# A graph network kernel whose gathers are paced by GpSimd: two halves of each round fetched row by row by SyncE and ScalarE

## The reference

```python
def _round(x, w, b, gamma, beta, src, dst, etype):
    h = jax.nn.relu(_bn(x, gamma, beta))          # N x 128
    h = jnp.einsum('nd,od->no', h, w) + b         # N x 640, one message row for each of 5 types
    msg = h.reshape(N, T, D)[src, etype]          # 200,000 rows of 128 floats
    return jax.ops.segment_sum(msg, dst, num_segments=N)
h_new = _round(features, w1, b1, g1, be1, src, dst, etype)
h_new = _round(h_new, w2, b2, g2, be2, src, dst, etype)
```

## Time and profile before

| | |
|---|---|
| median of 3 runs | 6475.83 us (6472.38 to 6478.03) |
| the profiled execution | 6482.43 us, of which its span is 6480.6 us |
| mean granted clock of TensorE | 0.727 |
| busy | POOL 71%, PE 64%, DVE 59%, ACT 25% |
| round 0: first to last gather | 164.4 to 2061.2 us |
| round 1: first to last gather | 2181.8 to 4074.4 us |
| second layer | from about 4085 us to the end |

### The profile page before, as it was taken

How to read it: one execution, slowest core, us unless ns; L and a number is a source line. 1 busy time by engine, 2 the same in 40 slices (tenths; PEclk the granted TensorE clock), 3 DMA queues, 4 the chain that set the end, 5 groups by cost and what they waited for, 6 DMA issues and landing times. The chain is left out here.

```text
span 6480.6 us, 66649 instructions
## 1 busy us (share of the span) xinstructions
PE 4158.0 (64%) x17271; PEld 2806.2 (43%) x17271; DVE 3822.2 (59%) x7438; ACT 1611.9 (25%) x3872; POOL 4619.0 (71%) x4787
## 2 busy tenths in 40 slices
PE   7445454544445645455454555778777889999898
PEld 4333343433334434334343444333323346666696
DVE  6544444443334777776676666544444457777698
ACT  4000000000001200000000000576666656666504
POOL 5777777777777677777777777577777777777604
PEclk9555555555556755655555676898898889999999
DMA  9211121212223521221222333333333356777696
GB/s 342 53 52 52 52 53 52 52 52 55 65 65 117 188 52 52 53 52 52 52 52 53 86 90 92 99 117 110 110 110 110 110 174 217 220 219 216 208 315 211
DMA packets 432604, 726.45 MB, mean 112 GB/s; under 512 B 104654, under 2 KB 206576, under 8 KB 431506
## 3 DMA queue, kind: packets, MB, share of 16 engines
q1 hardware_dynamic: 281652, 400.74, 19.7%
q0 software_dynamic: 150592, 321.58, 17.0%
HBM read 509.16 MB, written 212.75 MB: 111 GB/s over the span
## 5 line engine op out<-in xcount | busy, mean ns | idle before, releaser
L573 POOL DMA_INDIRECT edge_rows<-messages,idx_stage x1504 | 1446.1, 961 | 487.1 <-issue 457.9
L1658 PE MATMUL banks<-onehot,edge_rows 128*128 128x128 f32 x3008 | 715.9, 413 | 995.7 <-DMA edge_rows<-messages,idx_stage 960.8
L1658 PEld LDWEIGHTS banks<-onehot,edge_rows 128*128 128x128 f32 x3008 | 613.8, 303 | 1117.2 <-DMA edge_rows<-messages,idx_stage 1082.0
L630 POOL DMA_INDIRECT sorted_rows<-edge_rows,idx_stage x784 | 760.3, 970 | 276.3 <-issue 238.2
L630 POOL DMA_INDIRECT sorted_rows<-buf_a,idx_stage x784 | 760.5, 970 | 260.5 <-issue 241.4
L573 POOL DMA_INDIRECT buf_x<-messages,idx_stage x747 | 717.4, 960 | 227.7 <-issue 227.7
L573 POOL DMA_INDIRECT buf_a<-messages,idx_stage x747 | 714.5, 957 | 227.7 <-issue 227.7
L1040 DVE TENSOR_TENSOR buf_a<-buf_a,banks 128x128 f32 x375 | 108.1, 288 | 1044.3 <-PE banks L1658 1005.4
L689 ACT ACTIVATE h_stage<-banks,bn_shift,bn_scale 128x128 f32<-128x128 f32 x128 | 58.6, 458 | 2521.1 <-PE banks L1599 2521.1
L1658 PE MATMUL banks<-x_onehot,buf_x 128*128 128x128 f32 x1494 | 355.9, 413 | 490.6 <-DMA buf_x<-messages,idx_stage 490.5
L1658 PE MATMUL banks<-x_onehot,buf_a 128*128 128x128 f32 x1494 | 344.8, 403 | 459.9 <-DMA buf_a<-messages,idx_stage 459.5
(11 more groups left out here) (201 smaller groups left out, 7088.3 us busy)
## 6 DMA issues: line engine op xcount, KB each, us to landing
buf_a<-sorted_rows SPq DMA_DIRECT2D x593, 288.0 KB, 4.0
messages<-work SPq DMA_DIRECT2D x196, 320.0 KB
buf_a<-dst_rows SPq DMA_DIRECT2D x198, 256.0 KB
buf_a<-in_attr SPq DMA_DIRECT2D x198, 128.0 KB, 2.5
buf_a<-h_in SPq DMA_DIRECT2D x396, 64.0 KB
edge_rows<-messages,idx_stage POOLq DMA_INDIRECT x1504, 2.5
sorted_rows<-edge_rows,idx_stage POOLq DMA_INDIRECT x784
sorted_rows<-buf_a,idx_stage POOLq DMA_INDIRECT x784
```

What stands on the lines that cost most here:

```text
L573: nc.gpsimd.indirect_dma_start(gathered[p][h][:, t, :], None, source, bass.IndirectOffsetOnAxis(ap=idx_stage[:, h, t:t + 1], axis=0),).the ...
L630: nc.gpsimd.indirect_dma_start(sorted_rows, bass.IndirectOffsetOnAxis(ap=idx_stage[:, 2 * u + h, t:t + 1], axis=0), msg_halves[2 * u + h][ ...
L1658: last = nc.tensor.matmul(ps_sums[p][slot][j], rows_in_slot[:, j * GROUP_TILES + t, :], hot[:, j * GROUP_TILES + t, :], start=(t == 0), st ...
```

## The change

In each round, halves 140 and 141 (`FETCHED`) are not gathered by POOL. SP fetches half 140 and ACT half 141, each with one DMA for each of its 1,024 rows of 512 bytes, into two buffers of their own. Both load the row numbers from `msg_idx` four at a time. SP does its half in one go behind the stores of the messages; ACT does two partitions' rows (16 DMAs) after each of its 64 raw tiles. PE waits for the fetched half's own semaphore where it comes to it. Since the new buffers of round 1 take the place of `f_sb`, the memset of its last row and the loads of the attributes move to iteration 74 of round 1. A few semaphores are merged, with their counts carried on.

```diff
+FETCHED = (2 * 70, 2 * 71)
...
+        def fetch_tile(engine, kind, p, i, e, t):
+            rows = table[p].rearrange("n (t d) -> (n t) d", t=T)
+            at = nc.values_load_multi_w_load_instructions(
+                msg_idx[e:e + 1, FETCHED[i] * HALF_TILES + t:FETCHED[i] * HALF_TILES + t + 4], engines=[kind], min_val=0,
+                max_val=N * T - 1, skip_runtime_bounds_check_because="a source times the types plus a type")[1]
+            for j in range(4):
+                engine.dma_start(fetched[p][i][e:e + 1, t + j, :], rows[ds(at[j], 1), :]).then_inc(s_fetched[p][i], 16)
...
+            def fetch_half(p):
+                sp.wait_ge(s_setup, RANGE_LINKS + 2)
+                for q in range(SLOTS):
+                    sp.wait_ge(s_row_out[q], rows_out(p, q))
+                for e in range(P):
+                    for t in range(0, HALF_TILES, 4):
+                        fetch_tile(nc.sync, mybir.EngineType.SP, p, 0, e, t)
...
                 for n in range(TRANS_ITERS * SLOTS, BLOCKS):
                     store_messages(n, n % SLOTS)
 
+                fetch_half(rnd)
                 if rnd == 0:
 
                     sp.wait_ge(s_bias_split, 5)
...
             load_x(0)
+            sp.wait_ge(s_y, 1)
+            load_x(1)
             for h in range(2):
                 load_attributes(h, h)
-            sp.wait_ge(s_y, 1)
-            load_x(1)
...
                         pool.wait_ge(s_idx[p], r * GATHER_SLOTS + (h + 1))
+                        if r * GATHER_SLOTS + h + 2 * RAW_ITERS[p] in FETCHED:
+                            continue
...
+                act.wait_ge(s_setup, RANGE_LINKS + 2)
+                for q in range(SLOTS):
+                    act.wait_ge(s_row_out[q], rows_out(rnd, q))
                 for t in range(RAW_ITERS[rnd] * ITER_TILES):
...
                     nc.scalar.activation(h_stage[:, t % 2, :], ps_raw_turned, ACT.Relu,
                                          bias=bn_shift[:, 0:1], scale=bn_scale[:, 0:1]).then_inc(s_raw_h, 1)
+                    for e in range(2 * t, 2 * t + 2):
+                        for first in range(0, HALF_TILES, 4):
+                            fetch_tile(nc.scalar, mybir.EngineType.Activation, rnd, 1, e, first)
...
-                    pe.wait_ge(s_gather[2 * u + h][j], gathers(p, 2 * u + h, j, turn + 1))
+                    if source is None:
+                        pe.wait_ge(s_gather[slot][j], gathers(p, slot, j, turn + 1, after or isinstance(r2, int) and r2 > FETCH_TURN))
+                    else:
+                        pe.wait_ge(s_fetched[p][source], FETCH_ROWS)
```

More of the change, by code:

```diff
@@ L95 @@
 assert all(n % 2 == 0 and (2 * HALF_TILES // 2 + 1) * n + HALF_TILES + 2 <= CHUNK_ITERS + RAW_TILES for n in RAW_ITERS)
+assert RAW_TILES == P // 2
+assert all(2 * max(RAW_ITERS) <= k < 2 * CHUNK_ITERS for k in FETCHED)
 assert X_COLS * X_PARTS == N and X_COLS % BN_CHUNK == 0 and GROUPS % 4 == 0
@@ L194, in gnn_program @@
         raw_rows = [c[:, 0:RAW_TILES * P].rearrange("p (t n) -> p t n", n=P) for c in (buf_x, buf_a)]
+        fetched = [[c.rearrange("p (t n) -> p t n", t=HALF_TILES) for c in (
+            spare[:, at + half_cols * (2 + i):at + half_cols * (3 + i)] for i in range(len(FETCHED)))]
+            for spare, at in ((buf_x, RAW_ITERS[0] * ITER_TILES * P), (buf_a, RAW_ITERS[1] * ITER_TILES * P))]
         row_stages = [buf_a[:, i * WIDE:(i + 1) * WIDE] for i in range(6, CHUNKS)] + [
@@ L282, in gnn_program @@
         s_parts_in, s_bias_split = sem("bias_rows_in"), sem("bias_split")
-        s_bn, s_bn_sd = [sem(f"bn_step_{i}") for i in range(2)], [sem(f"bn_sd_{i}") for i in range(2)]
+        s_bn, s_bn_sd = [sem(f"bn_step_{i}") for i in range(2)], sem("bn_sd")
         s_h_ready = [sem(f"h_ready_{i}") for i in range(2)]
@@ L287, in gnn_program @@
         s_row_out = [sem(f"rows_out_{q}") for q in range(SLOTS)]
-        s_clear = [sem(f"acc_cleared_{i}") for i in range(2)]
+        s_clear = sem("acc_cleared")
         s_idx = [sem(f"idx_ready_{i}") for i in range(3)]
         s_gather = [[sem(f"gathered_{h}_{j}") for j in range(2)] for h in range(GATHER_SLOTS)]
+        s_fetched = [[sem(f"fetched_{p}_{i}") for i in range(len(FETCHED))] for p in range(2)]
         s_onehot = [sem(f"onehot_ready_{i}") for i in range(2)]
@@ L306, in gnn_program @@
         s_ps_iota, s_first = sem("iota_in_psum"), sem("first_places_step")
-        s_hot = [sem(f"high_onehot_{i}") for i in range(2)]
+        s_hot = sem("high_onehot")
         s_count, s_paired, s_picked, s_passed, s_placed, s_placed_out = (sem(n) for n in (
@@ L321, in gnn_program @@
         s_prod, s_turned = sem("products_ready"), sem("products_turned")
-        s_tagged, s_part = sem("rows_tagged"), sem("partitions_in_psum")
+        s_tagged = sem("rows_tagged")
         s_scat = [sem(f"scattered_{i}") for i in range(MSG_SLOTS)]
@@ L347, in rows_out, with gathers @@
             return ((each if stores is None else stores) + (1 + rnd * each)) * 16
-        def gathers(p, h, j, n):
+        def gathers(p, h, j, n, after=False):
             missing = 0 if h < GATHER_SLOTS - 1 else GROUP_TILES - LAST_TILES if j == 0 else GROUP_TILES
@@ L352, in gathers @@
             done = n * GROUP_TILES - (missing if isinstance(n, int) and n == turns_of[p] else 0)
-            return (done + p * (turns_of[0] * GROUP_TILES - missing)) * 16
+            skipped = GROUP_TILES * len([k for k in FETCHED if k % GATHER_SLOTS == h])
+            return (done + p * (turns_of[0] * GROUP_TILES - missing - skipped) - (skipped if after else 0)) * 16
+        FETCH_ROWS = COLS_HALF * 16
+        FETCH_TURN = FETCHED[0] // GATHER_SLOTS
+        assert all(k // GATHER_SLOTS == FETCH_TURN for k in FETCHED)
+        def fetch_tile(engine, kind, p, i, e, t):
[5 more added lines that the diff above has]
+                engine.dma_start(fetched[p][i][e:e + 1, t + j, :], rows[ds(at[j], 1), :]).then_inc(s_fetched[p][i], 16)
         def turns(engine, first, end, rolled=False):
@@ L418, in _ @@
             sp.wait_ge(s_short_out, 32)
-            for q in range(SLOTS):
-                sp.wait_ge(s_row_out[q], rows_out(1, q))
             def load_x(m):
@@ L610, in _ @@
             gather_raw(0)
-            nc.gpsimd.memset(buf_a[:, :], 0.0).then_inc(s_clear[0], 1)
+            nc.gpsimd.memset(buf_a[:, :], 0.0).then_inc(s_clear, 1)
             for rnd in range(2):
@@ L617, in _ @@
                     pool.wait_ge(s_closed, 2)
-                    nc.gpsimd.memset(buf_x[:, :], 0.0).then_inc(s_clear[1], 1)
+                    nc.gpsimd.memset(buf_x[:, :], 0.0).then_inc(s_clear, 1)
                 gather_pass(rnd, table[rnd].rearrange("n (t d) -> (n t) d", t=T),
@@ L668, in _ @@
                 act.wait_ge(s_bn[rnd], N // BN_CHUNK + 1)
-                nc.scalar.activation(bn_tmp[:, 0:1], bn_mv[:, 1:2], ACT.Sqrt, bias=eps_col[:, 0:1]).then_inc(s_bn_sd[rnd], 1)
+                nc.scalar.activation(bn_tmp[:, 0:1], bn_mv[:, 1:2], ACT.Sqrt, bias=eps_col[:, 0:1]).then_inc(s_bn_sd, 1)
                 act.wait_ge(s_bn[rnd], N // BN_CHUNK + 5)
@@ L888, in batch_norm @@
                 link(nc.vector.bn_aggr(bn_mv[:, :], bn_cols[rnd]))
-                dve.wait_ge(s_bn_sd[rnd], 1)
+                dve.wait_ge(s_bn_sd, rnd + 1)
                 dve.wait_ge(s_const_in, CONSTANTS * 16)
@@ L932, in build_high @@
                     src_high[:, ds(it * ITER_TILES + h * HALF_TILES, HALF_TILES)].unsqueeze(2).broadcast_to(shape),
-                    ALU.is_equal).then_inc(s_hot[p], 1)
+                    ALU.is_equal).then_inc(s_hot, 1)
             def count_lanes(k, h, j, i):
-                dve.wait_ge(s_hot[0], k + 1)
+                dve.wait_ge(s_hot, k + 1)
                 dve.wait_ge(s_count, k * 2 + (j + 1))
@@ L946, in pair_lanes @@
             def pair_lanes(k, h, i):
-                dve.wait_ge(s_hot[1], k + 1)
+                dve.wait_ge(s_hot, k + (2 * ITERS + 2))
                 dve.wait_ge(s_passed, k + (i + 1))
@@ L1259, in count_round, with filter_ones @@
                             round_half(0, buf_a, r, u, h, None, bases, False)
+            def filter_ones():
+                nc.vector.memset(f_sb[RBF:RBF + 1, :, :, :], 1.0).then_inc(s_cut, 1)
             def rank_beyond():
@@ L1266, in rank_beyond @@
                 dve.wait_ge(s_acc[1], GROUPS - 1 - 4 * RAW_ITERS[1] + SUMS)
+                filter_ones()
                 y_chunk(0)
@@ L1294, in round_pass @@
             def round_pass(p):
-                dve.wait_ge(s_clear[p], 1)
-                if p == 1:
-                    nc.vector.memset(f_sb[RBF:RBF + 1, :, :, :], 1.0).then_inc(s_cut, 1)
+                dve.wait_ge(s_clear, p + 1)
                 dve.wait_ge(s_row_ready[p], BLOCKS + SLOT3)
@@ L1437, in _ @@
             y_chunk(CHUNKS_IN)
-            nc.vector.tensor_copy(ps_part, part_f[:, :]).then_inc(s_part, 1)
+            nc.vector.tensor_copy(ps_part, part_f[:, :]).then_inc(s_ps_iota, 1)
             stage_cutoff(0, 0)
```

(18 more changed lines are left out.)

## The result

The changed kernel takes 6992.3 us (median of 6 runs, 6988.01 to 6996.79) against 6475.2 us before (median of 6, 6472.38 to 6478.03): ratio 1.0799, 95% interval 1.0789 to 1.081. It is 517 us slower; 7000 was forecast, 6955 to 7290 as the range. The profiled execution took 6996.8 us, 6995.0 of it span.

A forecast was written before the change was run, and what follows sets the result against it. POOL's gathers, 1.26 us apart, were taken to bound the kernel. A stall of + 564.5 us less 40.3 for saved gathers made + 524.2: 7000 us against the median, range 6955 to 7290.

The forecast's parts named there:

- The place of the loss: Round 0: PE waits for bias rows behind SP's fetch, POOL stops after 32 staged gathers; net + 524.2 us.
- Its size: Round 0: POOL's 33rd gather starts at 770.9 and not at 206.4, 564.5 us late.
- The term of SP's length: SP's round 0 fetch: 256 groups take 594 us, from 164.4 to 758.4.
- the chain of 12.5 us: Round 0: from SP's bias-row issue through PE's first sum to the copy staging half 12, 12.5 us.
- The price of a group: SP's fetch: one register load and four one-row DMAs with their register instructions take 2.32 us.
- the signs that the prediction named: Among them, on SP: register loads of 0.3 us, DMAs of 0.28 to 0.35 us, bias rows near 758.
- The gain: POOL, both rounds: 32 gathers fewer at 1.26 us, 40.3 us saved, 20.2 in each round.
- The argument for it: Round 0: half 142's row numbers are staged 6 us before POOL starts half 140, so the whole 40.3 us counts.
- The rivals: Faster or a tie, 0.02 and 0.01; dearer ACT fetches, 8580 us, 0.05; fetches waiting to land, about 11,800, 0.05.
- Fetches that follow one another only when landed: Rival on SP and ACT: each row takes 2.5 us, total about 11,800 us; chance 0.05.
- Faster: Rival: SP's 256 groups take under 70 us together, down to 6436 us; chance 0.02.
- Round 1: SP's fetch hidden, done near 2776 before half 140 is due at 3515; gathers' stretch 20 us shorter, no idle.

The follow-up runs named there:

- the version without a stall: SP's three bias-row loads put ahead of its round 0 fetch, all else as in the changed kernel: 6434.2 us, ratio 0.9938.
- the first two experiments: Against the changed kernel: bias-row loads ahead of SP's round 0 fetch, 6434.2 us; PE's wait for them moved to the last layer's output, 6432.8 us.

## Why the prediction was right

**The place of the loss.** As forecast: PE waits for `bias_rows` behind 1,024 fetches, POOL runs out of staged halves after 32 gathers. Shown by two runs that move one end of this wait each and lose the stall whole, and by one that halves it.

**Its size.** 564.5 us were forecast, 557.0 measured. The term of SP's length, 594 us, was 586.6 (register load at 163.84 us to the end of the last fetch at 750.4); the start and the chain of 12.5 us were right to 0.6 us.

**The price of a group was right by luck.** It was put together from a register load of 0.302 us and a DMA of 0.31. The lines of the changed kernel:

```profile
L369 SPq TENSOR_LOAD <-msg_idx x256: 457/561/731, 163.8 to 747.9; - x128
...
L373 SPq DMA_DIRECT2D buf_x<-messages x1024: 224/225/336, 164.5 to 750.2; - x171
```

The load is 0.26 us longer than its row of before, + 66 us over 256 groups. The DMA is 0.085 us shorter than the value taken, and shorter than each of the rows it was taken from the earlier trace rows, - 87 us. Slower first DMAs of a group (0.26), a few long loads and slightly longer gaps bring back some 13. So of the signs that the prediction named, neither the loads of 0.3 us nor the DMAs of 0.28 to 0.35 us came. Both prices came from the nearest rows, and each was wrong by more than a quarter. A better row for the load stood beside the one taken: the 0.531 us of DVE, which the prediction priced at 59 us more. The Trainium skill ("DMA: Bandwidth & Descriptors", section "Latency and other measured facts") names some 600 ns as the least for a register load; the prediction set this against the 302 ns on SP and went by the row. In the fetch it is 562, so the page was nearer for this use, though it isn't a least: the convolution's loads, in the changed kernel too, and the second of two loads in a row take 300 ns.

**The gain.** 40.3 us were forecast, in full. The gathers' stretches are 45.0 us shorter, of which about 40 are the 32 gathers and the rest is a slightly shorter distance between gathers in this execution (1.261 for 1.263 us in round 1). In the version without a stall 38.8 us reach the median. The argument for it had one half wrong. `FETCHED` is (2 * 70, 2 * 71), halves 140 and 142, and not 140 and 141 as the text ahead of the prediction has it: ACT fetches half 142, and POOL gathers 141. POOL's timeline in the changed kernel shows it, one half of eight gathers in `edge_rows` and one in `buf_x` where there were two each:

```profile
2057.79 0.95 POOL L601 DMA_INDIRECT buf_x<-messages,idx_stage  x1 [0.30 <-issue]
2059.04 0.95 POOL L601 DMA_INDIRECT edge_rows<-messages,idx_stage  x1 [0.30 <-issue]
...
2067.83 0.95 POOL L601 DMA_INDIRECT edge_rows<-messages,idx_stage  x1 [0.30 <-issue]
2069.09 0.95 POOL L601 DMA_INDIRECT buf_x<-messages,idx_stage  x1 [0.30 <-issue]
...
2079.15 0.95 POOL L601 DMA_INDIRECT edge_rows<-messages,idx_stage  x1 [0.30 <-issue]
```

So what had to be staged early was half 143, not 142: POOL starts it at 2069.09, and the copy of its numbers was made at 2064.55, 4.5 us before. The gain is the same, 16 gathers in each round.

**The rivals.** ACT's fetches cost 0.213 us a DMA, no more than SP's. In round 1 its raw tiles are 20.2 us apart with 8.6 us of fetches between:

```profile
3009.45 0.46 ACT L720 ACTIVATE h_stage<-banks,bn_shift,bn_scale 128x128 f32<-128x128 f32 x1 [19.64 <-PE banks L1636]
3010.11 8.56 ACTq L373 DMA_DIRECT2D buf_a<-messages  x16
3029.68 0.46 ACT L720 ACTIVATE h_stage<-banks,bn_shift,bn_scale 128x128 f32<-128x128 f32 x1 [19.77 <-PE banks L1636]
```

PE waits for ACT's raw tiles 3.1 us in all of round 0, right behind the stall, where POOL has gathers landed for it in advance. Fetches that follow one another only when landed: no, they are 0.41 us apart inside a group. Faster: only when the bias rows, or PE's wait for them, stand elsewhere, as the first two experiments show.

**Round 1.** SP is done with its fetch at 3300.6, issues the load of one chunk of x, and stands idle to 4117.9; its later loads of attributes and the moved memset show in no wait of POOL, as forecast.

## What to carry to other kernels

Work that is put on an idle queue pushes back everything behind it on that queue, also the things nobody thought of as urgent: look for each wait on what it issues later, and ask who is behind that wait. Here three small loads, needed only at the very end, were waited for at the start, and the order of three lines decided between 517 us lost and 39 gained. When an engine's issue rate sets the pace, rows fetched singly by idle engines do replace it, at 2.3 us for four rows, as long as each half has its deadline reckoned; and a sum that comes out right isn't proof of its prices.

## What the runs showed of the hardware

A DMA of one row of 512 bytes took ACT's queue 0.213 us, and SP's 0.225 in round 0 and 0.218 in round 1 of the changed kernel, 0.213 in round 0 of the version with the bias rows first; so the difference isn't one between the engines. 128 rows at a computed address took 0.343. In the page of the changed kernel a queue is new, q10, with 4096 packets for ACT's 2,048 fetches and 1.06 MB, so each fetch is one packet of data and one small one.

In SP's fetch a register load took 0.56 us behind a one-row fetch, 0.50 behind a wide DMA that itself stood behind such fetches, 0.50 behind a semaphore wait (the first load of the fetch), and 0.31 behind another load. There it did not depend on the tile, on the partition, or on whether the next instruction needed the number, and hardly on how many numbers were loaded (0.51 us for one). In the second layer's convolution SP's loads take 0.30 us, behind a wide DMA, behind a semaphore wait (0.297) and behind another load alike. No run here carries one case over into the other, so the reason is open.

During the stall TensorE's granted clock stood at 0.50, its lower level of 1.2 GHz, with nothing to do; the first eight matmuls behind it took 2.04 us, as long as the same ones before, and cost nothing beside POOL's pace.
